# The second conditioning weight loaded from ScalarE's queue instead of fifth on the sync queue

## The chip, the core and the metric

One core of a Trainium2 chip runs the whole kernel. The metric is device time in microseconds of one launch. Three runs of the kernel before took 242.04, 242.68 and 242.95 us; the median is 242.68 us.

## The reference

Two transformer layers of different kinds are applied to `x` (2 sequences of 512 rows, 128 features), both steered by one conditioning vector per sequence. The part that the change touches is the conditioning network of the first layer, a chain of five "bitlinear" products on a 2-row matrix. Each quantises its weight to -1, 0, 1 by the mean absolute value of the whole weight, and its input to 8 bits by the largest absolute value of the row:

```python
def _weight_quant(w):
    scale = 1.0 / jnp.clip(jnp.mean(jnp.abs(w)), 1e-05)
    return jnp.clip(jnp.round(w * scale), -1, 1) / scale
...
cc = jax.nn.silu(c)
h = _bitlinear(cc, wa0, na0)
h = _hgrn_mlp(h, wa1, na1, wa2, na2)
h = _bitlinear(h, wa3, na3, ba3)
h = _rmsnorm(h, wr, 1e-06)
params = _bitlinear(h, wa4, na4, ba4)
```

`params` holds shifts, scales and gates for everything that follows: a gated linear recurrence and a gated MLP (first layer), then causal attention with 16 heads of width 8 and a GELU MLP (second layer).

## The kernel before

The program is written out by hand for each engine, with semaphores between them; each engine does its instructions in the order of the text. SyncE (SP) issues nearly all loads from HBM in its first 8 us, one after the other on one queue. The order is: `crow` (the conditioning vectors and norm weights, 2 rows), `wa0`, `k_f` (constants), `ccol` (column vectors), `wa1`, `wa2`, `wa3`, then `x`, `wa4` in two halves, the main weights `mw`, the broadcast rows `brow`, one small row, the second layer's weights `lw` and the masks. `wa0` to `wa3` go into slices of one tile `cw`, each with its own semaphore `ld_cw[i]`. `wa1` is the largest of them, 128 x 1152 floats.

ScalarE (ACT) starts with the conditioning: it waits for `crow`, loads its function table, takes silu of `crow` (L520), then silu of `ccol` (L522, waits for `ld_col`), a sum of squares (L524), and then the sums of magnitudes of `wa0`, `wa1`, `wa2`, `wa3` in that order (L510, `magnitudes`, each waits for its own load). Then follows a sum of squares of the first product's output (L534), and the rounding of `wa1` (L540, L543) and `wa2` (L546, L549).

TensorE adds the sums over the partitions (L1431, `totals`). Its order is: total of `wa0`, transpose (L1437) and product (L1446) of the first bitlinear, total of `wa1`, total of `wa2` and `wa3` together, and then the second bitlinear. VectorE turns each total into the mean and its half (L883 to L886, `means`), quantises `wa0` (L910, L905) and the input (L964 to L967), quantises the transposed input (L983), scales a product's output into `cy` (L989, `row_of`), and in the order of its text the means of `wa1` stand between the first product's quantised input and its output. The large table work, the recurrence and the attention come later and are not changed.

Of the kernel before, what the change touches and what calls it, by code (L numbers as in the profile page):

```python
# [50 lines left out]
def _spans(*items):  # L51
    at, out = 0, {}
    for name, width in items:
        out[name] = (at, at + width)
        at += width
    return out, at

CW, CW_N = _spans(("wa0", D), ("wa1", 2 * ADA), ("wa2", ADAC * D), ("wa3", OUT6))
# [87 lines left out]
def build(nc, x, cond_w, wa4, cond_rows, main_w, l1_w, bcast_rows, cols, rows1, consts, out):  # L146
    with ExitStack() as ctx:
# [71 lines left out]
        cw = ct("cw", [P, CW_N])  # L219
# [46 lines left out]
        ld_cw = [ctx.enter_context(nc.semaphore(f"ld_cw{i}")) for i in range(4)]  # L266
# [23 lines left out]
        def tiles(b):  # L290
            return slice(b * NT, (b + 1) * NT)
# [46 lines left out]
        def stack_parts(queue, b, i, wanted=range(3)):  # L338

            stack, parts, done = ((QS[b], Q_PART, q_stacked[b]), (KS[b], K_PART, k_stacked[b]))[i]  # L340
            skip = HP if b == 0 else 0
            for want in wanted:
                queue.wait_ge((S["part0"], S["part1"], S["part2"])[want], 2 * b + i + 1)
                for slot in [s for s, p in enumerate(parts) if p == want]:
                    for half in range(2):
                        first = half * ROWS + slot * HD
                        queue.dma_start(stack[first:first + HD, skip:, :],  # L347
                                        part[b][i][want][half * ROWS + skip * HD:(half + 1) * ROWS, :]
                                        ).then_inc(done, 16)


        @block.sync
        def _(sp):
            sp.dma_start(crow[:, :], cond_rows).then_inc(S["ld_rows"], 16)
            for i, name in enumerate(("wa0", "wa1", "wa2", "wa3")):
                sp.dma_start(cw[:, slice(*CW[name])], cond_w[:, slice(*CW[name])]).then_inc(ld_cw[i], 16)
                if i == 0:
                    z = KC["kone"][1]
                    sp.dma_start(k_f[:, 0:z], consts[:, 0:z]).then_inc(S["ld_const"], 16)
                    sp.dma_start(ccol[:, :], cols).then_inc(S["ld_col"], 16)  # L360
            sp.dma_start(xs[:, :, :], x.rearrange("p (t d) -> p t d", d=D)).then_inc(S["ld_x"], 16)
            half = OC // 2
            for i in range(2):
                sp.dma_start(w4[:, half * i:half * (i + 1), :],
                             wa4[:, half * i * OUT6:half * (i + 1) * OUT6].rearrange("p (c n) -> p c n", n=OUT6)
                             ).then_inc(ld_w4[i], 16)
            sp.dma_start(mw[:, :], main_w).then_inc(S["ld_mainw"], 16)
            sp.dma_start(brow[:, :], bcast_rows.to_broadcast([P, BR_N])).then_inc(S["ld_bcast"], 16)
            sp.dma_start(row1[:, :], rows1).then_inc(S["ld_l1"], 16)
            sp.dma_start(lw[:, :], l1_w).then_inc(S["ld_l1"], 16)  # L370
            z = KC["kone"][1]
            sp.dma_start(k_f[:, z:], consts[:, z:]).then_inc(S["ld_masks"], 16)

            sp.wait_ge(S["stack_init"], B)
            stack_parts(sp, 0, 0)

            for n in range(B * NG):
                b, g = divmod(n, NG)
                sp.wait_ge(S["nm_copied"], n + 1)
                for half in range(2):  # L380
                    sp.dma_start(QS[b][half * ROWS + SROWS:half * ROWS + XROWS, 2 * g:2 * g + 2, :],
                                 nmT[n % 2][half * 3 * HG // 2:(half + 1) * 3 * HG // 2, :]
                                 ).then_inc(nm_stacked[n % 2], 16)
                if n < 2:
                    stack_parts(sp, 1, 0, ((0,), (1, 2))[n])
            for b in range(B):
                sp.wait_ge(S["y_ready"], b + 1)
                sp.dma_start(out[:, b * NT * D:(b + 1) * NT * D].rearrange("p (t d) -> p t d", d=D),
                             xs[:, tiles(b), :]).then_inc(S["stored"], 16)
            sp.wait_ge(S["stored"], 16 * B)  # L390
# [116 lines left out]
        def _(act):  # L507
# [6 lines left out]
            def load_table(fn, i):  # L514

                nc.scalar.activation(unused[:, i:i + 1], ones[:, 0:1], fn)

            act.wait_ge(S["consts_set"], 3)
            act.wait_ge(S["ld_rows"], 16)
            nc.scalar.activation(cy[:, 0:D], crow_of("c"), ACT.Silu).then_inc(S["silu_c"], 1)  # L520
# [15 lines left out]
            act.wait_ge(S["c_ssq"], 2)  # L536

            act.wait_ge(S["wa1_inv"], 1)
            wa1 = slice(*CW["wa1"])
            nc.scalar.activation(cw[:, wa1], cw[:, wa1], ACT.Copy, bias=MAGIC, scale=winv[:, 1:2]  # L540
                                 ).then_inc(S["wa1_magic"], 1)
            act.wait_ge(S["wa1_magic"], 1)
# [2 lines left out]
            wa2 = slice(*CW["wa2"])  # L545
# [310 lines left out]
        def _(dve):  # L856
# [103 lines left out]
            def c_quantise(k, i):  # L960

                n, chunks, _, w, _, _ = COND[k]
                dve.wait_ge(S["c_root"], i)
                then(V.scalar_tensor_tensor(cs_of(k, 4), cs_of(k, 1), CLIP / 127, cs_of(k, 2), ALU.mult, ALU.mult))  # L964
                then(V.scalar_tensor_tensor(cs_of(k, 5), cs_of(k, 3), 1.0 / 127, cs_of(k, 4), ALU.mult, ALU.max))
                then(V.reciprocal(cs_of(k, 6), cs_of(k, 5)))
                V.tensor_scalar(cq[:, 0:chunks * P], cu[:, 0:chunks * P], cs_of(k, 6), MAGIC, ALU.mult, ALU.add  # L967
                                ).then_inc(S["c_q"], 1)
# [6 lines left out]
            def c_scale(k):  # L975
                n, chunks, _, w, _, _ = COND[k]
                V.scalar_tensor_tensor(cs_of(k, 7), cs_of(k, 5), mean_of(w, B), cs_of(k, 2), ALU.mult, ALU.mult
                                       ).then_inc(S["c_scale"], 1)
# [446 lines left out]
        def _(pe):  # L1425
# [14 lines left out]
            def c_product(k):  # L1440
                n, chunks, _, w, n_out, bk = COND[k]
                pe.wait_ge(S["c_xq"], k + 1)
                for a in range(0, n_out, 512):
                    z = min(a + 512, n_out)
                    for c in range(chunks):
                        ins = T.matmul(bank(bk + a // 512)[0:B, 0:z - a], cxq[:, c, :], weights(w, c)[:, a:z],  # L1446
                                       start=(c == 0), stop=(c == chunks - 1))
                ins.then_inc(S["c_mm"], 1)
# [496 lines left out]
```

## Time and profile before

| | before |
|---|---|
| median of 3 runs | 242.68 us |
| profiled execution, device time | 243.1 us |
| its span (first to last instruction) | 241.3 us |
| around the span | 1.8 us |
| busy: TensorE, VectorE, ScalarE, GpSimd | 74%, 71%, 65%, 30% |
| granted TensorE clock, mean | 0.921 |
| loaded in slices 1 to 3 of 40 (6 to 24 us) | 360 to 421 GB/s |

A row of the timeline has the start, the duration, the engine, the line, the operation, what it writes and reads, and in brackets how long the engine was idle before it and what ended that. `SPq` is SyncE's queue issuing a DMA: its duration is that of the issue, not of the transfer. A row of the chain says what the end of the program was waiting for at that time. Names are those of the program; `PEld` is the weight load of a matmul.

### The profile page before, as it was taken

How to read it: one execution, taken by the hardware profiler on the slowest of the kernel's cores; microseconds unless marked ns; L12 is line 12 of the kernel's file. 1: busy time of each engine (PE TensorE's matmuls, PEld its weight loads, DVE VectorE, ACT ScalarE, POOL GpSimd, SP SyncE). 2: the span in 40 equal slices, each digit the busy share in tenths (PEclk: the TensorE clock that was granted, in tenths of full speed). 3: DMA queues.
4: the chain of work that ended last, by engine and by line, in shares of the span. 5: the costliest groups of instructions: out<-in, count | busy, mean ns of one | idle time of the engine just before them, and what ended most of it. 6: DMA issues, size and time to landing. Idle time of an engine off the chain costs nothing.

```text
span 241.3 us, 4480 instructions
## 1 busy us (share of the span) xinstructions
PE 178.5 (74%) x1621; PEld 108.3 (45%) x1625; DVE 170.2 (71%) x495; ACT 156.8 (65%) x344; POOL 71.9 (30%) x113
## 2 busy tenths in 40 slices
PE   0223457698764787729956986899999999889894
PEld 0202423687521333205634533546655655544763
DVE  3758888959886988696794498678877977442511
ACT  4798995775983866993425563567865875886241
POOL 8031231014523044495018694101101110130210
PEclk9999999555799799998998898699999999999999
DMA  5999000000000000000002350413000000000011
GB/s 142 421 418 360 26 0 0 0 3 1 0 1 0 3 0 0 1 0 0 3 0 67 71 117 13 66 37 39 3 2 5 3 5 5 2 3 0 0 46 43
DMA packets 4635, 11.50 MB, mean 48 GB/s; under 512 B 1283, under 2 KB 2788, under 8 KB 3974
## 3 DMA queue, kind: packets, MB, share of 16 engines
q1 hardware_dynamic: 3654, 10.03, 12.4%
q0 software_dynamic: 960, 1.19, 2.1%
q8 instruction: 13, 0.21, 0.4%
q14 instruction: 8, 0.07, 0.1%
HBM read 8.23 MB, written 0.52 MB: 36 GB/s over the span
## 4 chain that ended last, share of the span: by engine, by line
DVE 33%; PE 27%; ACT 17%; POOL 13%; issue 6%; DMA 3%; SPq 1%; ACTq 0%; DVEq 0%; POOLq 0%
DVE negmax L1374 8%; PE ps L1771 6%; PE ps L1528 5%; POOL uh L460 4%; POOL KS L347 3%; ACT PT L804 2%; ACT fg L653 2%; PE ps L1710 2%; PE ps L1807 2%; ACT xhat L602 2%; DMA cw<-in_cond_w 2%; DVE mx L1265 2%; POOL rms L404 2%; ACT junk L510 2%; DVE u L1158 2%
## 5 line engine op out<-in xcount | busy, mean ns | idle before, releaser
L1374 DVE TENSOR_REDUCE negmax<-ps 128x1 f32<-128x384 f32 (+3 forms) x96 | 51.2, 593 | 13.7 <-PE ps L1712 13.5
L804 ACT ACTIVATE PT<-ps 128x1024 f32<-128x1024 f32 x40 | 39.5, 1031 | 20.3 <-PE ps L1757 20.2
L1710 PE MATMUL ps<-KS,QS 48*128 48x128 bf16 (+3 forms) x128 | 31.3, 314 | 1.5 <-DVE negmax L1374 0.6
L1539 PE MATMUL ps<-k_b 128*128 128x512 bf16 x100 | 25.7, 412 | 8.3 <-DVE prod L1312 4.4
L1751 PE MATMUL ps<-QS,KS 51*128 51x512 bf16 (+3 forms) x128 | 24.3, 311 | 1.7 <-DMA QS<-nmT 1.7
L1711 PE MATMUL ps<-k_b 64*128 64x128 bf16 x128 | 23.6, 224 | 0.0
L1712 PE MATMUL ps<-k_b 64*128 64x64 bf16 x128 | 21.3, 195 | 0.0
L1771 PE MATMUL ps<-PT,V 128*9 128x512 f32 (+3 forms) x256 | 20.4, 434 | 0.0
L404 POOL TENSOR_TENSOR rstd<-veps,mhalf 128x4 f32<-128x4 f32 x8 | 8.4, 1050 | 39.5 <-DVE veps L932 37.1
L1539 PEld LDWEIGHTS ps<-k_b 128*128 128x128 bf16 x100 | 10.1, 106 | 22.3 <-DVE prod L1312 4.9
L404 POOL TENSOR_TENSOR rms<-vms,mhalf 128x4 f32<-128x4 f32 x10 | 10.2, 1026 | 31.5 <-DVE vms L1132 31.5
L1757 PE MATMUL ps<-k_b 64*128 64x128 bf16 x128 | 18.4, 223 | 0.0
L1754 PE MATMUL ps<-k_b 64*128 64x64 bf16 x128 | 17.3, 195 | 0.0
L486 POOL CAST nmpart<-negmax 128x16 bf16<-128x16 f32 x8 | 1.6, 198 | 52.1 <-DVE negmax L1374 52.1
L1710 PEld LDWEIGHTS ps<-KS,QS 48*128 48x128 bf16 x128 | 11.0, 95 | 10.3 <-DVE negmax L1374 7.6
L1528 PE MATMUL ps<-k_f,u 128*128 128x128 f32 x40 | 8.1, 366 | 9.2 <-ACT u L704 4.8
L347 POOL DMA_DIRECT2D KS<-part x24 | 13.4, 564 | 2.6 <-ACT part L778 2.0
L1712 PEld LDWEIGHTS ps<-k_b 64*128 64x128 bf16 x128 | 11.7, 99 | 4.4 <-issue 0.6
L1711 PEld LDWEIGHTS ps<-k_b 64*128 64x128 bf16 x128 | 11.5, 99 | 0.0
L1528 PEld LDWEIGHTS ps<-k_f,u 128*128 128x128 f32 x40 | 6.5, 191 | 11.1 <-DVE u L1158 6.1
L460 POOL TENSOR_TENSOR uh<-prod,brow 128x512 f32<-128x512 f32 x8 | 9.9, 1276 | 4.5 <-DVE prod L1312 4.5
L1751 PEld LDWEIGHTS ps<-QS,KS 51*128 51x128 bf16 x128 | 9.1, 96 | 3.9 <-issue 2.3
(242 smaller groups left out, 459.2 us busy)
## 6 DMA issues: line engine op xcount, KB each, us to landing
w<-in_wa SPq DMA_DIRECT2D x2, 1152.0 KB, 9.6
lw<-in_l_w SPq DMA_DIRECT2D x1, 1280.0 KB
brow<-in_bcast_rows SPq DMA_DIRECT2D x1, 1152.0 KB, 15.4
mw<-in_main_w SPq DMA_DIRECT2D x1, 1024.0 KB, 12.4
KS<-part POOLq DMA_DIRECT2D x12, 64.0 KB, 3.4
QS<-part SPq DMA_DIRECT2D x12, 64.0 KB
cw<-in_cond_w SPq DMA_DIRECT2D x1, 576.0 KB, 4.5
xs<-in_x SPq DMA_DIRECT2D x1, 512.0 KB, 6.1
```

The lines of the kernel that those rows point to most:

```text
L347: queue.dma_start(stack[first:first + HD, skip:, :], part[b][i][want][half * ROWS + skip * HD:(half + 1) * ROWS, :]).then_inc(done, 16)
L404: return nc.gpsimd.tensor_tensor(r, v, mhalf[0:v.shape[0], 0:v.shape[-1]], ALU.pow)
L460: nc.gpsimd.tensor_tensor(uh[b][:, t, :], prod[b][t % 2][:, :], brow_of("nm2"), ALU.mult).then_inc(S["uh_raw"], 1)
L804: nc.scalar.activation(PT[n % 2][:, s, :], bank(2 * (use % 2), 2), ACT.Exp).then_inc(S["p_ready"], 1)
L1374: V.tensor_reduce(negmax[n % 2][:, qt, h0:h0 + nh], bank(S_BANKS[k % 3])[:, 0:nh * w].rearrange("p (h w) -> p h w", w=w), AX.X, ALU.max, n ...
L1528: ins = T.transpose(dst[:, tok(t)], src(t), ident)
L1539: T.matmul(bank(bk).rearrange("p (r n) -> p r n", n=P), ident_b, ident_b.unsqueeze(1).to_broadcast([P, NT, P]), start=True, stop=True)
L1710: T.matmul(dst, QS[b][rows, h, tok(qt)], KS[b][rows, h, 0:w], start=True, stop=False)
L1711: T.matmul(dst[:, w - P:w], k_of("pickLo", r), k_of("maskQlo", r), start=False, stop=False)
L1712: ins = T.matmul(dst[:, w - P // 2:w], k_of("pickHi", r), k_of("maskQhi", r), start=False, stop=True)
L1751: T.matmul(dsts[half], KS[b][rows, h, tok(kt)], QS[b][rows, h, kt * P:L], start=True, stop=False)
L1771: ins = T.matmul(bank(PV_BANKS[n])[32 * j:32 * j + HD + 1, kt * P:L], V1[b][:, kt, g * HG + j, :], src, start=(kt == 0), stop=(kt == 2))
```

## The change

`wa1` is left out of SyncE's loop, and ScalarE issues its load as the first instruction of its own block, ahead of its wait for `crow`. The semaphore `ld_cw[1]` and all waits stay as they are.

```diff
         @block.sync
         def _(sp):
             sp.dma_start(crow[:, :], cond_rows).then_inc(S["ld_rows"], 16)
-            for i, name in enumerate(("wa0", "wa1", "wa2", "wa3")):
+            for i, name in ((0, "wa0"), (2, "wa2"), (3, "wa3")):
                 sp.dma_start(cw[:, slice(*CW[name])], cond_w[:, slice(*CW[name])]).then_inc(ld_cw[i], 16)
...
+            wa1 = slice(*CW["wa1"])
+            act.dma_start(cw[:, wa1], cond_w[:, wa1]).then_inc(ld_cw[1], 16)
             act.wait_ge(S["consts_set"], 3)
             act.wait_ge(S["ld_rows"], 16)
...
-            wa1 = slice(*CW["wa1"])
             nc.scalar.activation(cw[:, wa1], cw[:, wa1], ACT.Copy, bias=MAGIC, scale=winv[:, 1:2]
                                  ).then_inc(S["wa1_magic"], 1)
```

SyncE's first issues before, in order (the three slices of `cw` are `wa0`, 128x128, `wa1`, 128x1152, `wa2`, 128x640, and `wa3`, 128x768):

```order
L354 DMA crow<-in_cond_rows 2x1408
L356 DMA cw<-in_cond_w 128x128
L359 DMA k_f<-in_consts 128x145
L360 DMA ccol<-in_cols 128x32
L356 DMA cw<-in_cond_w 128x1152
L356 DMA cw<-in_cond_w 128x640
L356 DMA cw<-in_cond_w 128x768
L361 DMA xs<-in_x 128x1024
```

and SyncE's first issues now:

```order
L354 DMA crow<-in_cond_rows 2x1408
L356 DMA cw<-in_cond_w 128x128
L359 DMA k_f<-in_consts 128x145
L360 DMA ccol<-in_cols 128x32
L356 DMA cw<-in_cond_w 128x640
L356 DMA cw<-in_cond_w 128x768
L361 DMA xs<-in_x 128x1024
```

The 128x1152 load is gone, and every load from `wa2` on stands one place earlier. On ScalarE the start of the program changes so (the lines of the text are two or one further on from here):

```order
 L506 UNCONDITIONAL_BRANCH
-L520 ACT_TABLE_LOAD
-L520 ACTIVATE cy<-crow 2x128
-L522 ACTIVATE scT<-ccol 128x2
-L524 ACTIVATE junk,cs<-cy 2x128
+L519 DMA cw<-in_cond_w 128x1152
+L522 ACT_TABLE_LOAD
+L522 ACTIVATE cy<-crow 2x128
+L524 ACTIVATE scT<-ccol 128x2
+L526 ACTIVATE junk,cs<-cy 2x128
 L510 ACTIVATE junk,wsum<-cw 128x128
 L510 ACTIVATE junk,wsum<-cw 128x1152
```

The load stands ahead of the table load, and nothing else changes its place. TensorE, VectorE and GpSimd keep their order.

## Rows read from the trace of the kernel before

**Rows 1.** The page's part 4: shares of the whole chain by engine.

```profile
DVE 33%; PE 27%; ACT 17%; POOL 13%; issue 6%; DMA 3%; SPq 1%; ACTq 0%; DVEq 0%; POOLq 0%
```

**Rows 2.** The chain in 0 to 18 us: start us, us, what.

```profile
7.03 1.26 ACT junk L510 x2
...
8.40 0.84 ACT junk L510 x2
...
9.35 0.94 ACT junk L510 x2
```

**Rows 3.** Timeline, 0 to 12 us, ScalarE's rows.

```profile
2.48 1.28 ACT L520 ACT_TABLE_LOAD   x1 [2.48 <-DMA crow<-in_cond_rows]
...
3.77 0.31 ACT L520 ACTIVATE cy<-crow 2x128 f32<-2x128 f32 x1
...
4.03 0.20 ACT L522 ACTIVATE scT<-ccol 128x2 f32<-128x2 f32 x1
...
4.61 0.31 ACT L510 ACTIVATE junk<-cw 128x128 f32<-128x128 f32 x1
...
7.03 1.16 ACT L510 ACTIVATE junk<-cw 128x1152 f32<-128x1152 f32 x1 [2.02 <-DMA cw<-in_cond_w]
...
10.37 0.31 ACT L534 ACTIVATE junk<-cy 2x128 f32<-2x128 f32 x1
```

**Rows 4.** Timeline, 5 to 10.5 us, TensorE and VectorE up to the first product's output.

```profile
5.16 0.56 PE L1431 MATMUL ps<-wsum,ones 128*128 128x1 f32 x2 [5.16 <-ACT junk L510]
...
8.45 0.26 PE L1446 MATMUL ps<-cwq,cxq 128*2 128x128 bf16 x1 [0.25 <-DVE cxq L983]
8.64 0.50 PEld L1431 LDWEIGHTS ps<-wsum,ones 128*128 128x128 f32 x2
...
9.86 0.34 DVE L989 TENSOR_SCALAR cy<-ps,cs 2x128 f32<-2x128 f32 x1
```

**Rows 5.** Timeline, 22 to 23 us: the same step with ScalarE idle before it.

```profile
22.05 0.34 DVE L989 TENSOR_SCALAR cy<-ps,cs 2x128 f32<-2x128 f32 x1 [0.20 <-PE ps L1446]
22.43 0.31 ACT L573 ACTIVATE junk<-cy 2x128 f32<-2x128 f32 x1 [0.46 <-DVE cy L989]
```

**Rows 6.** Timeline, SyncE's queue: start and duration of issues.

```profile
0.74 0.35 SPq L354 DMA_DIRECT2D crow<-in_cond_rows  x1
...
1.15 0.37 SPq L356 DMA_DIRECT2D cw<-in_cond_w  x1
...
2.03 0.43 SPq L360 DMA_DIRECT2D ccol<-in_cols  x1
...
2.50 1.38 SPq L356 DMA_DIRECT2D cw<-in_cond_w  x3
```

**Rows 7.** The page's part 6: KB of each load, us from issue to landing.

```profile
w<-in_wa SPq DMA_DIRECT2D x2, 1152.0 KB, 9.6
...
cw<-in_cond_w SPq DMA_DIRECT2D x1, 576.0 KB, 4.5
...
cw<-in_cond_w SPq DMA_DIRECT2D x1, 384.0 KB, 5.3
...
cw<-in_cond_w SPq DMA_DIRECT2D x1, 320.0 KB, 4.8
...
cw<-in_cond_w SPq DMA_DIRECT2D x1, 64.0 KB, 1.8
...
ccol<-in_cols SPq DMA_DIRECT2D x1, 16.0 KB, 2.0
```

**Rows 8.** A stretch of 0.5 us: busy of five engines, then PEclk, DMA share, GB/s.

```profile
2.00:2.50 0.50, 0.00 (x0) 0.00 (x0) 0.47 (x1) 0.02 (x1) 0.50 (x1) 1.00 0.37 108
```

**Rows 9.** Timeline, 4 to 23 us: issue of `wa4` (w), first uses of `wa4` and `mw`.

```profile
4.40 1.26 SPq L364 DMA_DIRECT2D w<-in_wa  x2
...
14.65 0.83 ACT L510 ACTIVATE junk<-w 128x768 f32<-128x768 f32 x1
...
22.86 0.31 ACT L510 ACTIVATE junk<-mw 128x128 f32<-128x128 f32 x1
```

## The prediction

> **What bounds the kernel now.** I read the shares of the chain first: transfers are 3% of it and SyncE's queue 1% [rows 1], so a change to a load can be worth 7 or 8 us at most, and only at the start. Then I read the chain's own steps there. It runs from SyncE's issues into the load of `wa1`, then through the sums of magnitudes of `wa1`, `wa2` and `wa3` on ScalarE without a gap: 7.03 to 8.29, 8.40 to 9.24, 9.35 to 10.29 us [rows 2]. Third, ScalarE's timeline: it stands idle for 2.02 us before the sum of `wa1`, and the load ends that idle time [rows 3]. That is the wait the change goes for, and by the chain alone it looks like 2.02 us.
>
> But a chain shows one of several paths that may end at almost the same time, so the fourth reading is the step where ScalarE's sums are first needed together with something else. After the sum of `wa3` comes L534, at 10.37 us [rows 3]. It reads `cy`, which VectorE writes from 9.86 to 10.20 us [rows 4]. So when ScalarE was free at 10.29 us, its input had been there for 0.09 us only. Behind `cy` stands a second chain: total of `wa0` on TensorE at 5.16, released by ScalarE's first sum, then VectorE's quantising, the product L1446 at 8.45, the total of `wa1` at 8.64 and its means, then `cy` [rows 4]. Does this second chain wait for `wa1`'s load anywhere? The only place is the total of `wa1`. Its sum was ready at 8.29 [rows 2]; TensorE begins it at 8.64, with no idle time shown before it, right behind a product that could not start before 8.45 [rows 4]. So no. The second chain would have ended at 10.20 us with `wa1` landed at any time before about 7.3 us.
>
> **The change, part by part.**
>
> *The load moves to ScalarE.* SyncE's first issue is at 0.74 us [rows 6]; ScalarE does nothing before 2.48 us, where `crow` lands and its table load starts [rows 3]. An issue takes 0.35 to 0.46 us (1.38 for three) [rows 6], so ScalarE is done with it by about 1.2 us, and even with a start one issue later, at 1.6. Its own cost is 0: the wait for `crow` hides it with 0.9 us or more to spare. Without that cover it would cost its 0.46.
>
> *`wa1` lands earlier.* From 2.50 to about 0.74 us is 1.76 us. With the same 4.5 us from issue to landing [rows 7] it lands at 5.25 instead of 7.01. ScalarE begins the sum of `wa0` at 4.61 [rows 3] and is ready for `wa1` some 0.5 us later, so the wait shrinks from 2.02 to a few tenths and the sum ends at about 5.3 + 1.26 = 6.5 us.
>
> *`wa2`, `wa3` and the rest are issued one place earlier*, 0.46 us. The same bytes stand ahead of them on the same DMA engines, so I take no more than the slot and, as the other bound, nothing. `wa2` landed at 2.96 + 4.8 = 7.8 and `wa3` at 3.42 + 5.3 = 8.7 us [rows 6, 7]. What is late next on ScalarE is then `wa2`: even with nothing gained its sum runs 7.8 to 8.6, and that of `wa3` 8.8 to 9.7. So ScalarE is free at 9.7 us at the latest, against 10.29.
>
> *What is left of it.* L534 then waits for `cy`, ready at 10.20. A twin of this step, with ScalarE idle before it, starts 0.04 us after `cy` is complete (22.05 + 0.34 to 22.43) [rows 5]. So L534 starts at 10.24 instead of 10.37: gain 0.13 us. Of 2.02 us removed, 1.89 turn into later waits of ScalarE (for `wa2`, `wa3` and `cy`). The 0.13 goes on to the end, since from L534 the chain goes through ScalarE's rounding of `wa1` and the later loads have room: `wa4` is issued in two halves from 4.40 on, with a median of 9.6 us to landing, so the first half lands at about 14.0 [rows 7, 9]; it is first used at 14.65, and its load moves earlier too. `mw` is used at 22.86 [rows 9]. If that cover of `wa4` were gone it would give back the 0.13, no more.
>
> *What the early load does to the small ones.* This is the part with a price. Before, `crow`, `wa0`, `k_f` and `ccol` had the DMA engines to themselves: 2.0 to 2.5 us shows a busy share of 0.37 at 108 GB/s [rows 8]. Now `wa1`, 576 KB, runs through the same stretch. What slack do they have? `wa0` lands at 1.15 + 1.8 = 2.95 and is used at 4.61: 1.66 us [rows 3, 6, 7]. `crow` ends ScalarE's wait at 2.48: none. `ccol` is issued at 2.03 and lands at 4.03, and L522 starts at 4.03: none either [rows 3, 6, 7]. L522 stands in ScalarE's order ahead of the sum of `wa0`, the head of the second chain. So each 0.1 us by which `crow` or `ccol` is late is 0.1 us on the total of `wa0`, on `cy`, and on the end. No row shows two queues at once, so I bound the delay. Lower end: 0, the DMA engines had idle time in that stretch [rows 8] and the small loads are spread thin. Upper end: a small load waits for all of `wa1`; `crow` would land with it at 5.25 instead of 2.48, 2.77 us late. The nearest row is an issue slot: if SyncE and ScalarE take turns at issuing, each later SyncE issue slips by one, 0.43 us [rows 6], and `ccol` lands at 4.46. I take that, 0.43.
>
> The sum: 0.43 − 0.13 = +0.30 us. On the profiled execution that is 241.3 to 241.6 of span, 243.1 to 243.4 with the 1.8 around it; that execution lies 0.4 above the median, and on the median of 242.68 it is 243.0 us. From both sides: −0.13 gives 242.55, +2.64 gives 245.3.
>
> *A rule against the change.* Before, SyncE's issues follow each other every 0.4 to 0.5 us with nobody beside them [rows 6]. The Trainium skill, "Perfetto Trace Analysis", section "DMA Instruction — HWDGE (DVE, Sync)", says that a descriptor generator is locked by one sequencer at a time; by it the simultaneous issues queue up, one slot or two on the way to `ccol`, which is the sign of my 0.43. No trace so far shows it. "DMA: Bandwidth & Descriptors", section "Queues, rings and completion order", says that a completion count on a DMA engine lands only after all earlier writes of that engine, from every queue. By it `ccol` could not be signalled before the part of `wa1` that ran ahead of it; that is the third case below, and no trace shows this either.
>
> **The rivals.**
>
> *A: forecast.* The small loads slip by 0.2 to 0.8 us, the 2.02 us wait goes, ScalarE waits later. 242.75 to 243.4, at 243.0. Chance 0.44.
>
> *B: nothing slips.* For it: the idle share of the DMA engines [rows 8]. Against it: zero slack of two loads. Time 242.68 − 0.13 = 242.55. Chance 0.30.
>
> *C: the slower side, `wa1` in front of `crow` or `ccol`.* The place is L522 on ScalarE (or the table load before it), the price is the delay of that load less 0.13, and it decides from a delay of 1.35 us on (1.21 + 0.13). For it: `wa1` needs 4.5 us from issue to landing [rows 7], now 0.74 to 5.25, and the landings of `crow` (2.48) and `ccol` (4.03) both fall into that time [rows 3]. Against it: `crow` is issued as early as `wa1` can be and has 2 rows, and `ccol` comes when most of `wa1` should be through. Time: a delay of 1.35 to 2.77 us gives 243.9 to 245.3; I put it at a delay of 1.75, 244.3. Chance 0.12.
>
> *D: the wait is worth itself.* The second chain gets shorter too, for instance because the total of `wa1` was waiting after all. Then 2.02 us come off: 240.7. Against it: the two times at 8.29 and 8.64, and `wa0`'s own steps, which are no shorter. Chance 0.06.
>
> *E: the change does not do what it says:* ScalarE's load gets served after SyncE's, `wa1` lands near 7 us as before, 242.7. Against it: the idle share of the DMA engines at 2.0 to 2.5 us [rows 8]. Chance 0.08.
>
> **How the numbers follow.** About 0.5%, 1.21 us, is what can be told from no change: below 241.47 is faster, above 243.89 slower. The runs themselves lie 242.04 to 242.95, 0.4 to 0.6 on either side. A, B and E lie within, 0.82; C is slower, 0.12; D is faster, 0.06. The likeliest case gives 243.0. The range leaves out D and most of C: from B less the spread of the runs, 242.0, to A plus that spread and the low end of C, 244.1.
>
> **What would show it.** Right: the idle time of 2.0 us before the sum of `wa1` shrinks under 0.5; ScalarE instead shows idle time before the sums of `wa2` or `wa3` or before L534; L534 starts about 0.04 us after `cy`, and `cy` is written no earlier than 9.86 us. A delay of the small loads shows as a later table load (`crow`, 2.48) or as idle time before L522 (`ccol`, 4.03), with the sum of `wa0` behind 4.61 by as much. Wrong: `cy` complete well before 10.2 us, or L534 more than 0.3 us ahead of its 10.37; a delay over 1.35 us at L522; a difference of the whole that the start of L534 does not show.

## The result, and the profile after

| | before | changed |
|---|---|---|
| median | 242.58 us (5 runs, 242.04 to 242.95) | 244.12 us (5 runs, 243.40 to 244.27) |
| ratio to before | | 1.0061, 95% interval 1.0040 to 1.0082 |
| profiled execution: device time, span | 243.1, 241.3 us | 244.12, 242.3 us |
| first product's output `cy` written from | 9.86 us | 11.26 us |
| sum of squares behind it (L534, now L536) starts | 10.37 us | 11.63 us |

The kernel became 0.6% slower, about 1.5 us (0.0061 x 242.58), at the upper end of the range. The load the change moves did come earlier, and the wait for it is gone. What replaced it is seen on ScalarE, in the timeline of the changed kernel, 0 to 12 us:

```profile
0.74 0.36 SPq L354 DMA_DIRECT2D crow<-in_cond_rows  x1
0.74 0.38 ACTq L519 DMA_DIRECT2D cw<-in_cond_w  x1
...
1.16 0.37 SPq L356 DMA_DIRECT2D cw<-in_cond_w  x1
...
2.03 0.43 SPq L360 DMA_DIRECT2D ccol<-in_cols  x1
...
3.08 1.28 ACT L522 ACT_TABLE_LOAD   x1 [3.08 <-DMA crow<-in_cond_rows]
...
4.38 0.31 ACT L522 ACTIVATE cy<-crow 2x128 f32<-2x128 f32 x1
...
5.42 0.20 ACT L524 ACTIVATE scT<-ccol 128x2 f32<-128x2 f32 x1 [0.74 <-DMA ccol<-in_cols]
...
6.00 0.31 ACT L510 ACTIVATE junk<-cw 128x128 f32<-128x128 f32 x1
...
6.52 1.16 ACT L510 ACTIVATE junk<-cw 128x1152 f32<-128x1152 f32 x1
...
11.26 0.34 DVE L990 TENSOR_SCALAR cy<-ps,cs 2x128 f32<-2x128 f32 x1
11.63 0.31 ACT L536 ACTIVATE junk<-cy 2x128 f32<-2x128 f32 x1 [1.86 <-DVE cy L990]
```

Against [rows 3]: the 2.02 us of idle time before the sum of `wa1` are gone. `crow` comes 0.60 us later (3.08 for 2.48) in this execution, and the silu of `ccol` starts at 5.42 instead of 4.03, 1.39 us late, after waiting for its load. The sum of `wa0` behind it is late by the same 1.39 (6.00 for 4.61), `cy` by 1.40. Only at the end does ScalarE give the foreseen 0.13 back: L536 is 1.26 us late. It now waits 1.86 us for `cy`.

SyncE's issues are where they were [rows 6]: 0.74, 1.16, 2.03 us. So the small loads are not issued late; they move late. The page's part 6 for the changed kernel (KB, us from issue to landing):

```profile
cw<-in_cond_w ACTq DMA_DIRECT2D x1, 576.0 KB, 3.9
...
k_f<-in_consts SPq DMA_DIRECT2D x1, 72.5 KB, 3.5
cw<-in_cond_w SPq DMA_DIRECT2D x1, 64.0 KB, 3.7
...
ccol<-in_cols SPq DMA_DIRECT2D x1, 16.0 KB, 3.4
```

`wa0` took 1.8 us before and takes 3.7 now, `ccol` 2.0 and 3.4 [rows 7]. Why, is shown by the DMA queues in short stretches. Here is the stretch 1.5 to 3.5 us of the changed kernel, queue by queue (packets, MB, share of the 16 engines; q10 is ScalarE's queue, q1 SyncE's):

```profile
q10 hardware_dynamic: 97, 0.45, 80.3%
q1 hardware_dynamic: 4, 0.01, 1.5%
```

In the same stretch before, SyncE's queue moved everything small:

```profile
q1 hardware_dynamic: 403, 0.16, 36.6%
```

SyncE's queue got 4 packets through in 2 us, although `wa0`, `k_f` and `ccol` had all been issued by 2.46 us. Its packets come in numbers only from 3.5 us on (112 to 4.0 us, 260 to 4.5 us), when `wa1` is nearly through. The two queues don't share evenly here: nearly all of `wa1` goes first, and the small loads behind `crow` come after it. The rows count the packets of all engines together and don't say where the small loads were kept, on the DMA engines or on the way to them.

From L536 on the delay travels unchanged for a while (1.28 us at the first `par`, 36.88 to 38.16) and comes out as 1.0 at the last store of this profile, with other granted clocks in between; the timed runs give 1.5, with an interval of 1.0 to 2.0.

### The profile page after: what moved, and what is told of

Same layout as the page of the kernel before. It is cut to its first block, busy times and chain, and to the rows that moved or that the text cites. A ratio compares the mean times of both kernels' runs of the same rounds, so it can differ in the third digit from the quotient of the medians.

```text
span 242.3 us, 4480 instructions
## 1 busy us (share of the span) xinstructions
PE 179.9 (74%) x1621; PEld 108.1 (45%) x1625; DVE 170.1 (70%) x495; ACT 157.0 (65%) x344; POOL 72.0 (30%) x113
## 4 chain that ended last, share of the span: by engine, by line
DVE 32%; PE 31%; ACT 14%; POOL 11%; issue 7%; DMA 2%; SPq 1%; DVEq 0%; ACTq 0%; POOLq 0%
DVE negmax L1375 6%; PE ps L1772 6%; POOL KS L347 5%; PE ps L1529 5%; PE ps L1540 3%; PE ps L1711 2%; ACT fg L654 2%; ACT PT L805 2%; PE ps L1808 2%; DVE mx L1266 2%; PE ps L1752 2%; DVE prod L1313 2%; PE ps L1802 2%; DVE bnst L926 1%; DMA ccol<-in_cols 1%
## 5 line engine op out<-in xcount | busy, mean ns | idle before, releaser
L1540 PE MATMUL ps<-k_b 128*128 128x512 bf16 x100 | 28.8, 452 | 7.1 <-DVE prod L1313 4.4
L1711 PE MATMUL ps<-KS,QS 48*128 48x128 bf16 (+3 forms) x128 | 32.1, 321 | 1.3 <-DVE negmax L1375 0.8
L1752 PE MATMUL ps<-QS,KS 51*128 51x512 bf16 (+3 forms) x128 | 24.8, 315 | 1.6 <-DMA QS<-nmT 1.6
L1712 PE MATMUL ps<-k_b 64*128 64x128 bf16 x128 | 24.1, 229 | 0.0
L1713 PE MATMUL ps<-k_b 64*128 64x64 bf16 x128 | 21.6, 198 | 0.0
L1540 PEld LDWEIGHTS ps<-k_b 128*128 128x128 bf16 x100 | 11.1, 115 | 23.4 <-issue 7.9
L1758 PE MATMUL ps<-k_b 64*128 64x128 bf16 x128 | 18.9, 225 | 0.0
L1755 PE MATMUL ps<-k_b 64*128 64x64 bf16 x128 | 17.7, 197 | 0.0
L1529 PE MATMUL ps<-k_f,u 128*128 128x128 f32 x40 | 8.6, 381 | 9.9 <-DVE u L1159 5.2
L1711 PEld LDWEIGHTS ps<-KS,QS 48*128 48x128 bf16 x128 | 11.1, 96 | 10.5 <-DVE negmax L1375 7.9
L1713 PEld LDWEIGHTS ps<-k_b 64*128 64x128 bf16 x128 | 12.0, 102 | 4.6 <-issue 0.8
L1712 PEld LDWEIGHTS ps<-k_b 64*128 64x128 bf16 x128 | 11.7, 101 | 0.0
```

What stands on the lines that cost most here:

```text
L1529: ins = T.transpose(dst[:, tok(t)], src(t), ident)
L1540: T.matmul(bank(bk).rearrange("p (r n) -> p r n", n=P), ident_b, ident_b.unsqueeze(1).to_broadcast([P, NT, P]), start=True, stop=True)
L1711: T.matmul(dst, QS[b][rows, h, tok(qt)], KS[b][rows, h, 0:w], start=True, stop=False)
L1712: T.matmul(dst[:, w - P:w], k_of("pickLo", r), k_of("maskQlo", r), start=False, stop=False)
L1713: ins = T.matmul(dst[:, w - P // 2:w], k_of("pickHi", r), k_of("maskQhi", r), start=False, stop=True)
L1752: T.matmul(dsts[half], KS[b][rows, h, tok(kt)], QS[b][rows, h, kt * P:L], start=True, stop=False)
```

## The experiments

The last column is the ratio of the medians to the kernel before on the same chip. The two columns ahead of it are times in us from one profiled execution of each kernel: the start of the silu of `ccol`, and, under "L534", that of the sum of squares behind `cy`, whatever its line number there. Before they are 4.03 and 10.37. "Issue later" rests on 4 timed runs, the changed kernel on 5, each of the others on 9 to 12.

| kernel | `scT` from | L534 | ratio (95% interval) |
|---|---|---|---|
| changed | 5.42 | 11.63 | 1.0061 (1.0040 to 1.0082) |
| issue later | 6.01 | 12.22 | 1.0098 (1.0068 to 1.0129) |
| first 64 KB only | 4.18 | 10.42 | 1.0015 (0.9999 to 1.0031) |
| half of `wa1` | 5.04 | 11.24 | 1.0041 (1.0020 to 1.0062) |
| `wa1` second on SyncE | 5.71 | 11.92 | 1.0064 (1.0039 to 1.0090) |
| `scT` behind the sums | 9.57 | 10.54 | 1.0015 (0.9996 to 1.0035) |
| `ccol` ahead on ScalarE | 3.98 | 10.63 | 1.0032 (1.0006 to 1.0058) |
| no wait for `wa1` | 4.00 | 10.29 | 0.9999 (0.9973 to 1.0025) |
| early table | 3.99 | 9.93 | 0.9988 (0.9961 to 1.0015) |
| early table, small loads split | 4.16 | 9.47 | 0.9958 (0.9937 to 0.9979) |

**Is it the second queue or the bytes? The first 64 KB.** ScalarE loads a ninth of `wa1`, SyncE the rest in the old place; the sum of `wa1` waits for both parts.

```diff
-            act.dma_start(cw[:, wa1], cond_w[:, wa1]).then_inc(ld_cw[1], 16)
+            act.dma_start(cw[:, wa1.start:wa1.start + D], cond_w[:, wa1.start:wa1.start + D]).then_inc(ld_cw[1], 16)
...
+                    sp.dma_start(cw[:, a1 + D:z1], cond_w[:, a1 + D:z1]).then_inc(ld_cw[1], 16)
```

> ScalarE's first instruction loads only the first 128 of the 1152 columns of wa1 (64 KB instead of 576); SyncE loads the other 512 KB in wa1's old place. T1 (bytes): an eighth of the bytes, crow at 2.5 to 2.7, scT at 4.0 to 4.3, sum of squares of the first product near 10.4 to 10.6, time within 0.3 us of before (242.6 to 242.9). T2 (the second queue by itself, at its first use): crow at 3.08 and scT at 5.4 as in the changed kernel, sum of squares at 11.6, 244.1.

Measured: `crow` at 2.67, `scT` at 4.18, L534 at 10.42. Each is within 0.2 us of before, so a second queue in use costs next to nothing by itself. Half of `wa1` on ScalarE, and the other half on SyncE in the old place, gives the step between:

```diff
-            act.dma_start(cw[:, wa1.start:wa1.start + D], cond_w[:, wa1.start:wa1.start + D]).then_inc(ld_cw[1], 16)
+            act.dma_start(cw[:, wa1.start:wa1.start + ADA], cond_w[:, wa1.start:wa1.start + ADA]).then_inc(ld_cw[1], 16)
```

> ScalarE's first instruction loads half of wa1 (576 columns, 288 KB), SyncE the other half in wa1's old place. Theory T3 (a small load waits for what reached the engines before it): ccol's delay lies between that of 64 KB (scT at 4.18) and of 576 KB (5.42), at 4.5 to 4.9; sum of squares of the first product at 10.7 to 11.1, time 242.8 to 243.5. If only the full size did harm, scT stays near 4.2 and the time at before.

Measured: `scT` at 5.04 and L534 at 11.24, in between as said but 0.14 us above both ranges I had given, and the median of 243.82 is above its range too. The delay of `scT` is 0.15, 1.01 and 1.39 us for 64, 288 and 576 KB: it grows with the bytes, and not in proportion to them. The landing of ScalarE's part does not set it alone: the half landed at 0.74 + 2.9 = 3.6 us, `ccol` only at 5.0. In between its rows (128 B each) still trickle: packets under 512 B are 99, 40 and 16 in the half microseconds from 3.5, 4.0 and 4.5 us. SyncE's own half of `wa1`, issued at 2.51, moves beside them; that it slows them is likely, but not shown.

**Issue `wa1` later.** ScalarE issues it behind its wait for the constants.

```diff
-            act.dma_start(cw[:, wa1], cond_w[:, wa1]).then_inc(ld_cw[1], 16)
             act.wait_ge(S["consts_set"], 3)
+            act.dma_start(cw[:, wa1], cond_w[:, wa1]).then_inc(ld_cw[1], 16)
             act.wait_ge(S["ld_rows"], 16)
```

> Changed kernel, but ScalarE issues the load of wa1 after its wait for GpSimd's constants (about 1.65 us) and ahead of its wait for crow, instead of at 0.74 us. Theory T1 (wa1's bytes on the DMA engines hold up the small loads that run at the same time): crow, already moving by then, is back near 2.5 us (changed kernel 3.08), ccol is still late, scT starts at 4.7 to 5.4 us, the sum of squares of the first product starts at 10.9 to 11.6. Theory T2 (a second queue in use makes SyncE's loads slow whatever it carries and whenever it is filled): scT stays at 5.4, and the sum at 11.6 us. Time by T1 243.0 to 243.8, by T2 244.1.

The waits moved as in these rows of its timeline:

```profile
1.16 0.37 SPq L356 DMA_DIRECT2D cw<-in_cond_w  x1
1.56 0.43 SPq L359 DMA_DIRECT2D k_f<-in_consts  x1
1.68 0.37 ACTq L520 DMA_DIRECT2D cw<-in_cond_w  x1
2.04 0.43 SPq L360 DMA_DIRECT2D ccol<-in_cols  x1
2.09 1.28 ACT L522 ACT_TABLE_LOAD   x1 [2.09 <-POOL cu L397]
...
6.01 0.20 ACT L524 ACTIVATE scT<-ccol 128x2 f32<-128x2 f32 x1 [2.32 <-DMA ccol<-in_cols]
```

`ccol` is later than ever, and so is the time: both are outside what I expected of either theory (5.4 us and 244.1 at most; measured 6.01 and 244.45). What is spared is `wa0`, issued half a microsecond ahead of `wa1`: 2.0 us to landing, 1.8 before. `k_f`, issued 0.12 us ahead of `wa1`, takes 4.0, and `ccol`, behind it, 4.0. A later `wa1` goes with a later `ccol`: `wa1` lands at 1.68 + 4.1 = 5.8 us here, at 4.6 in the changed kernel. That formed the third theory: order of arrival, a whole load at a time. (The table load starts before `crow` is waited for here, so this run does not show when `crow` landed.)

The queues' packets of this run bear out the order and not the "whole load at a time". In 3.0 to 5.0 us:

```profile
q10 hardware_dynamic: 123, 0.55, 73.3%
q1 hardware_dynamic: 119, 0.06, 14.9%
```

Of the packets in this stretch 93 have 512 B to 2 KB, the size of `k_f`'s rows (580 B). So `k_f`, whose packets had begun, went on beside `wa1`, but slowly. `ccol`'s small rows come behind both: packets under 512 B are 30 in these 2 us and 146 in the next 0.5.

**The same order on one queue.** All loads on SyncE, `wa1` in second place.

```diff
-            for i, name in enumerate(("wa0", "wa1", "wa2", "wa3")):
+            for i, name in ((1, "wa1"), (0, "wa0"), (2, "wa2"), (3, "wa3")):
```

> Kernel before with all loads on SyncE, but wa1 second, right behind crow and ahead of wa0, k_f and ccol. Theory T3 (the DMA engines take what reaches them in order of arrival, a whole load at a time, whichever queue it came on): the same harm without a second queue. wa0, k_f and ccol begin only when wa1 is through, wa1 starts one slot later than in the changed kernel, so scT starts at 5.5 to 6.1 us, the sum of squares of the first product at 11.7 to 12.3, time 244.2 to 245. Theory T2' (the harm comes from ScalarE's queue having precedence over SyncE's): the slow part is gone, wa0 to ccol come as they do before, slipped by one issue slot at most; sum of squares at 10.4 to 10.8, time 242.5 to 243. crow, issued first and alone, is at 2.48 by either.

```profile
2.46 1.28 ACT L520 ACT_TABLE_LOAD   x1 [2.46 <-DMA crow<-in_cond_rows]
...
3.75 0.31 ACT L520 ACTIVATE cy<-crow 2x128 f32<-2x128 f32 x1
...
5.71 0.20 ACT L522 ACTIVATE scT<-ccol 128x2 f32<-128x2 f32 x1 [1.65 <-DMA ccol<-in_cols]
```

Measured as the third theory has it: `scT` at 5.71, L534 at 11.92, ratio 1.0064. Nothing is on ScalarE's queue, and the harm is that of the changed kernel. So the harm needs no second queue: 576 KB ahead of three small loads are enough. By itself this does not exclude that ScalarE's queue also had precedence in the changed kernel. Against that speak the rows above, in which SyncE's queue moved 119 packets while `wa1` ran on ScalarE's.

**Which small load binds.** First the silu of `ccol` was moved behind the four sums:

```diff
-            act.wait_ge(S["ld_col"], 16)
-            nc.scalar.activation(scT[:, :], ccol[:, slice(*CC["cT"])], ACT.Silu).then_inc(S["silu_c"], 1)
...
                 magnitudes(cw[:, slice(*CW[name])], name)
 
+            act.wait_ge(S["ld_col"], 16)
+            nc.scalar.activation(scT[:, :], ccol[:, slice(*CC["cT"])], ACT.Silu).then_inc(S["silu_c"], 1)
```

> Changed kernel with the silu of ccol moved behind the four sums of magnitudes, so that ScalarE no longer waits for ccol ahead of the sum of wa0. If ccol's delay is 0.79 of the 1.39 us and crow's is the rest, the sum of wa0 starts at about 5.1 (bounded by wa0's own landing at 1.16 + 3.7 = 4.9 and k_f's at 5.1) instead of 6.00, and the sum of squares of the first product at 10.7 to 10.8 instead of 11.63; time 0.8 to 0.9 under the changed kernel, 243.2. If instead crow alone set the delay (the wait at scT being hidden in it), nothing moves: 244.1.

Of the 1.26 us at L534, 1.09 came back (10.54, somewhat more than the 10.7 to 10.8 expected). The sum of `wa0` now waits for its own load:

```profile
2.48 1.28 ACT L522 ACT_TABLE_LOAD   x1 [2.48 <-DMA crow<-in_cond_rows]
...
4.93 0.31 ACT L510 ACTIVATE junk<-cw 128x128 f32<-128x128 f32 x1 [0.41 <-DMA cw<-in_cond_w]
```

And `crow` is not late at all here. My split of the 1.39 into 0.60 for `crow` and 0.79 for `ccol` was wrong. A second profile of both kernels bears on it.

> The changed kernel once more, for one look: crow was 0.60 us late in its first profile, and not late at all in the profile of the kernel with the silu of ccol moved, although both issue the same loads in the same order. If the two queues' first loads race (both issued at 0.74 us), crow's landing scatters between 2.48 and 3.08 from execution to execution; ccol's landing stays at 5.2 to 5.4, since it waits for the end of wa1 either way, and the sum of squares of the first product stays at 11.4 to 11.7.

> The kernel with the silu of ccol behind the sums once more, for one look. If crow's landing is a race: 2.48 or 3.08 or between; in either case the sum of wa0 is bound by wa0's landing at 4.8 to 5.0 and the sum of squares of the first product stays at 10.5 to 10.8.

Measured: changed kernel with `crow` at 2.58, `scT` at 5.39, L534 at 11.60; the other with `crow` at 2.48, L534 at 10.53. `crow` scatters over 0 to 0.6 us from execution to execution (the two first issues are 0.01 us apart), and this doesn't matter, since `ccol` ends the same wait at 5.4 either way. `ccol` is the load that binds in the changed kernel. Put ahead of `wa1` on ScalarE's queue it no longer does:

```diff
+            act.dma_start(ccol[:, :], cols).then_inc(S["ld_col"], 16)
             act.dma_start(cw[:, wa1], cond_w[:, wa1]).then_inc(ld_cw[1], 16)
```

(and out of SyncE's list.)

> Changed kernel with the load of ccol (16 KB) moved from SyncE to ScalarE's queue, ahead of wa1. T1, with the loads of one queue begun in order: ccol is there by about 3.1, before the silu of crow ends, so scT no longer waits; crow stays late by 0.4 to 0.6 (its queue still shares the engines with wa1), sum of wa0 at 5.1 to 5.2 (then bound by crow and by wa0, whose landing at 4.9 stays), sum of squares of the first product at 10.7 to 10.9, 243.1 to 243.3. T2: ccol is as late as before on either queue, 244.

```profile
3.98 0.19 ACT L524 ACTIVATE scT<-ccol 128x2 f32<-128x2 f32 x1
...
5.55 0.56 PE L1432 MATMUL ps<-wsum,ones 128*128 128x1 f32 x2 [5.55 <-DMA k_f<-in_consts]
```

`scT` is back at 3.98, and the next small load takes over: TensorE's total of `wa0`, at 5.55 for 5.16 [rows 4], now waits for `k_f`. Three of the four small loads bound something in turn.

**What was the wait worth?** The kernel before with no load moved; the sum of magnitudes "of `wa1`" reads a constant column instead, so the mean of `wa1` is left out.

```diff
-                act.wait_ge(ld_cw[i], 16)
+                if i != 1:
+                    act.wait_ge(ld_cw[i], 16)
...
-                magnitudes(cw[:, slice(*CW[name])], name)
+                magnitudes(cw[:, slice(*CW[name])] if i != 1 else ones[:, 0:1].to_broadcast([P, 2 * ADA]), name)
+            act.wait_ge(ld_cw[1], 16)
```

> Kernel before, loads untouched, but the sum of magnitudes of wa1 reads a constant column repeated 1152 times instead of wa1, and so doesn't wait for its load (ScalarE waits for wa1 later, where it is long there). This leaves the mean of wa1 out of the computation. It removes the 2.02 us wait alone, without moving a byte. Theory of the two chains: the sum of squares of the first product goes from 10.37 to 10.24 us, since the first product's output still comes at 10.20; time 242.3, not to be told from before. Rival (the wait is worth itself): it goes to about 8.4 us and the time to 240.4.

```profile
5.11 1.16 ACT L510 ACTIVATE junk<-ones 128x1152 f32<-128x1152 f32 x1
...
8.03 0.74 ACT L510 ACTIVATE junk<-cw 128x640 f32<-128x640 f32 x1 [1.67 <-DMA cw<-in_cond_w]
...
8.66 0.50 PEld L1433 LDWEIGHTS ps<-wsum,ones 128*128 128x128 f32 x2
...
10.29 0.31 ACT L536 ACTIVATE junk<-cy 2x128 f32<-2x128 f32 x1 [0.36 <-DVE cy L991]
```

The sum is ready 1.9 us earlier, the total of `wa1` still runs at 8.66, and L534 moves from 10.37 to 10.29. The 2.02 us wait was worth 0.08 us there, and 1.67 us of it reappear before the sum of `wa2`. The timed ratio, 0.9999, agrees; its interval is 0.6 us to either side, which excludes a gain of 2 us.

**A version that beats both.** Taking the wait out of the first chain gained nothing, so here both chains are shortened. First the second one alone, loads untouched: the function table is loaded before `crow` is there, and the silu of `ccol` stands behind the sum of `wa0`.

```diff
+            act.wait_ge(S["consts_set"], 1)
+            load_table(ACT.Silu, 3)
             act.wait_ge(S["consts_set"], 3)
             act.wait_ge(S["ld_rows"], 16)
...
                 magnitudes(cw[:, slice(*CW[name])], name)
+                if i == 0:
+                    act.wait_ge(S["ld_col"], 16)
+                    nc.scalar.activation(scT[:, :], ccol[:, slice(*CC["cT"])], ACT.Silu).then_inc(S["silu_c"], 1)
```

> Kernel before, loads untouched, with ScalarE's function table loaded before crow is there and the silu of ccol behind the sum of wa0. The second chain starts about 1.2 us earlier (total of wa0 at 3.9 instead of 5.16, then bound by k_f's landing). Now the load of wa1 is what binds: sums of wa1, wa2, wa3 still end at 10.29, the product's output at about 9.9, the sum of squares stays at 10.3 to 10.4. So no gain: 242.2 to 242.6. If the second chain alone bounds the kernel, it goes to about 9.1 and the time to 241.3.

L534 at 9.93; ratio 0.9988, not to be told from no change. The total of `wa0` moved from 5.16 to 3.86, and the sums on ScalarE bind again, as expected. They ended 0.45 us earlier than in the profile of before, since `wa1` landed in 4.1 us here and not in 4.5. SyncE issues the same loads in the same order in both, and in the kernel without the wait it took 4.7, so this may be the spread of one load between executions; these single profiles don't show it. With it L534 came 0.4 us ahead of the range I had given. Then the loads too, but the small ones first: SyncE keeps `crow`, `wa0`, `wa1`, `wa2`, `wa3` in this order, and ScalarE issues the other two small ones.

```diff
-                if i == 0:
-                    z = KC["kone"][1]
-                    sp.dma_start(k_f[:, 0:z], consts[:, 0:z]).then_inc(S["ld_const"], 16)
-                    sp.dma_start(ccol[:, :], cols).then_inc(S["ld_col"], 16)
...
+            z = KC["kone"][1]
+            act.dma_start(k_f[:, 0:z], consts[:, 0:z]).then_inc(S["ld_const"], 16)
+            act.dma_start(ccol[:, :], cols).then_inc(S["ld_col"], 16)
             act.wait_ge(S["consts_set"], 1)
             load_table(ACT.Silu, 3)
```

> As the early-table kernel, and the small loads are spread over both queues: SyncE issues crow, wa0, wa1, wa2, wa3, ScalarE k_f and ccol as its first two instructions. So wa1 is issued at 1.56 instead of 2.50 us, and still behind all small loads. Theory: both chains are shortened, wa1 lands at about 6.0, sums end at 9.3 to 9.4, the product's output at about 9.3, sum of squares at 9.4 to 9.7 instead of 10.37: time 241.5 to 241.9, under before by 0.7 to 1.0. If arrival order is not what counts and k_f or ccol on ScalarE's queue meet wa1 all the same, the total of wa0 waits for k_f at 4.5 or later, and the gain is under 0.3.

```profile
0.73 0.39 ACTq L515 DMA_DIRECT2D k_f<-in_consts  x1
...
1.15 0.45 ACTq L516 DMA_DIRECT2D ccol<-in_cols  x1
1.15 1.78 SPq L356 DMA_DIRECT2D cw<-in_cond_w  x4
...
5.91 1.16 ACT L506 ACTIVATE junk<-cw 128x1152 f32<-128x1152 f32 x1 [1.56 <-DMA cw<-in_cond_w]
...
9.47 0.31 ACT L536 ACTIVATE junk<-cy 2x128 f32<-2x128 f32 x1 [0.32 <-DVE cy L991]
```

`wa1` is summed from 5.91 on instead of 7.03, no small load is waited for, L534 starts at 9.47. Median 241.48 us, ratio 0.9958 (0.9937 to 0.9979): 1.0 us faster than before and, by the two ratios, 2.5 us faster than the changed kernel. The split of the small loads was not run without the early table, so its own share is not shown.

## Why the prediction was right, and where it was not

*The two chains:* right. The wait of 2.02 us was worth 0.13 us by the prediction and 0.08 with nothing else touched. In the changed kernel the difference between the delay of `scT` (1.39) and that of L536 (1.26) is the same 0.13. Where the 2.02 us went came out otherwise there: no new wait before `wa2` or `wa3`, but 0.60 more for `crow`, 0.74 for `ccol` and 1.86 for `cy`. The waits for `wa2` or `wa3` show only where the small loads no longer bind (1.67, 1.07 and 0.73 us in three of the other kernels).

*ScalarE's own issue is free:* right. It runs at 0.74 to 1.12 us, over before anything that ScalarE waits for.

*`wa1` lands earlier:* right, and by more: 0.74 + 3.9 = 4.6, where 5.25 was expected.

*The later loads have room:* right, no new wait for them appeared. They were first used some 1.25 us later than before (`wa4` at 15.90 for 14.65), so this was no hard test.

*The small loads:* this is the step that failed, in its size and in its reason. I took one issue slot, 0.43 us, for `ccol`, "if SyncE and ScalarE take turns at issuing". It measured 1.39. The reason was wrong as well: SyncE's issues did not move (1.16 and 2.03 us). The delay arises behind the issue: `ccol`'s packets move only when most of the bytes of `wa1` have gone. With 1.39 − 0.13 the sum is +1.26 on L536, against +0.30 in the forecast. That is rival C with its mechanism at `ccol`, just past the 1.35 us from which it was to decide; I gave it 0.12. Its argument against, that most of `wa1` would be through when `ccol` comes, was false: `wa1` landed at 4.6, `ccol` came at 2.0. The figure for it was at hand: 4.5 us from issue to landing [rows 7]. By that I should have put `ccol` behind 5.25, 1.2 us late, and forecast +1.1.

*The outcome:* the median of 244.12 lies 0.02 above the stated upper end of 244.1 in plain microseconds, against 243.0 as the likeliest. That it comes so near the range is luck and no merit of the sum: the sum was short by 0.96 us, and the upper end had the spread of the runs and the low end of rival C in it. The direction was right, the forecast that the time can't be told from before was not: 244.12 is above the 243.89 from which the prediction calls it slower, and the interval of the ratio, 1.0040 to 1.0082, excludes 1. One of its own signs of being wrong came true as well, a delay over 1.35 us at L522. Rivals B, D and E are excluded by the same rows (`ccol` slipped; `cy` is later, not earlier; `wa1` did land early).

*The two cited rules:* simultaneous issues showed no turn-taking, those of 0.36 and 0.38 us ran side by side from 0.74. The Trainium skill, "Perfetto Trace Analysis", section "DMA Instruction — HWDGE (DVE, Sync)", has the generator locked for one sequencer at a time; no wait of that kind can be seen in these rows. On the order of the loads, the Trainium skill, "DMA: Bandwidth & Descriptors", section "Queues, rings and completion order", says that a DMA engine goes round its queues and changes only at the end of a packet, which holds several descriptors. The 97 packets against 4 would agree with that if an engine's share of a load is one such packet; no run here shows how a load is divided. The other rule that the Trainium skill gives in this section, that completion comes after all earlier writes, was not in the main what held `ccol` up: its packets themselves moved late. Only 2 packets under 512 B moved up to 3.5 us (`ccol`'s rows are 128 B), while before 125 moved in 3.0 to 3.5 us alone.

Not settled: where between the issue and the DMA engines the small loads were kept, and why half of `wa1` costs as much as 1.01 of the 1.39 us. The timed ratios of several kernels lie 0.2 to 0.6 us above their shift at L534 (1.5 for 1.26, 0.8 for 0.26), but each of these differences lies inside the interval of its ratio, so there may be nothing to explain.

## What to carry to other kernels

An idle time in the chain is worth only what the next meeting point with another chain leaves: look there how long the other input had been ready (here 0.09 us). Moving the 576 KB load to the front, on either queue, put the small loads issued after it behind its bytes: they took 3.2 to 3.7 us to land instead of 1.8 to 2.3. So issue first the small loads whose landing has no slack, and let the large one follow. Spreading the small ones over two queues lets the large one be issued earlier; the last kernel did this, together with the early table, and gained 1.0 us.

## What the hardware showed unexpectedly

Two issues from SyncE and ScalarE at the same time cost each other nothing (0.36 and 0.38 us, both from 0.74), but in the changed kernel their loads hardly interleave: 97 packets of the one and 4 of the other in 2 us. That is not so of every pair of loads: with `wa1` issued at 1.68 us the two queues moved 123 and 119 packets in the same 2 us. There `k_f`, issued 0.12 us ahead of the large load, was slowed by it (4.0 us instead of 2.3), and `wa0`, issued 0.52 us ahead, was not (2.0 for 1.8). `crow`, issued within 0.01 us of it, came at 2.48, 2.58 or 3.08 us. In the last kernel ScalarE's queue carries `k_f` and `ccol` while SyncE's carries the rest: they take 2.0 and 2.5 us and land at about 2.7 and 3.7 us, and neither is waited for.
